# A two-layer graph transformer in one pipeline: value products and output projections of two units in one run in every second step

## The reference

```python
# layer 0
nx = ln(x, ln1_g, ln1_b); q, k, v = nx @ wq + bq, nx @ wk + bk, nx @ wv + bv
scores = q @ k.T / sqrt(32) + where(adj > 0, 0.1 * adj * adj, -inf)
out = softmax(scores) @ v
x1 = x + (out @ wo + bo)
x2 = x1 + gelu(ln(x1, ln2_g, ln2_b) @ w1 + b1) @ w2 + b2
# layer 1
q, k, v = x2 @ Wq + bq, x2 @ Wk + bk, x2 @ Wv + bv
h = softmax(where(adj == 0, -inf, q @ k.T / sqrt(32))) @ v
y = ln(h @ Wo + bo + x2, gamma, beta)
```

## Time and profile before

| what | value |
|---|---|
| median of 3 runs | 2196.2 us (2194.52 to 2197.47) |
| profiled execution, its own time | 2197.36 us |
| its span in the profile | 2195.3 us |
| mean granted TensorE clock | 0.988 |
| busy: PE, PEld, DVE, ACT, POOL | 2150.0, 1859.5, 1802.1, 1683.8, 1155.7 us |

### The profile page before, as it was taken

How to read it: one execution, slowest core, us unless ns; L and a number is a source line. 1 busy time by engine, 2 the same in 40 slices (tenths; PEclk the granted TensorE clock), 3 DMA queues, 4 the chain that set the end, 5 groups by cost and what they waited for, 6 DMA issues and landing times.

```text
span 2195.3 us, 58908 instructions
## 1 busy us (share of the span) xinstructions
PE 2150.0 (98%) x20300; PEld 1859.5 (85%) x20300; DVE 1802.1 (82%) x8414; ACT 1683.8 (77%) x5646; POOL 1155.7 (53%) x1266
## 2 busy tenths in 40 slices
PE   8899999999999999999999999999999999999986
PEld 6688888888888888888888888888888888888875
DVE  6688888888888888888888888888888888888774
ACT  5578787778777778877778877788877787877773
POOL 4345655445655455655455555455555455555454
PEclk9999999999999999999999999999999999999997
DMA  4010111011111001111101110101111001110000
GB/s 128 25 35 28 40 33 40 23 31 35 40 33 36 27 28 38 37 36 31 32 28 38 34 39 31 33 26 40 33 40 31 30 28 40 33 40 29 22 14 17
DMA packets 94309, 75.74 MB, mean 35 GB/s; under 512 B 8129, under 2 KB 93761, under 8 KB 94017
## 3 DMA queue, kind: packets, MB, share of 16 engines
q1 hardware_dynamic: 94016, 71.99, 10.7%
HBM read 55.20 MB, written 16.78 MB: 33 GB/s over the span
## 4 chain that ended last, share of the span: by engine, by line
PE 95%; DVE 2%; issue 1%; ACT 1%; POOL 0%; DMA 0%; SPq 0%; POOLq 0%; DVEq 0%
PE p_bank L1124 67%; PE p_heads L1221 10%; PE p_heads L1208 8%; PE p_bank L1240 7%; PE p_bank L1143 4%; ACT scores L650 1%; DVE normed L883 0%; DVE x_two L768 0%; DVE probs_t L920 0%; ACT normed L661 0%; DMA scores<-in_L_gnn_wk 0%; DVE scores L861 0%; DVE adj_c L814 0%; SPq L440 0%; POOL w_up L374 0%
## 5 line engine op out<-in xcount | busy, mean ns | idle before, releaser
L650 ACT ACTIVATE scores<-scores,negmax 128x128 f32<-128x128 f32 x2048 | 793.7, 393 | 25.4 <-DVE negmax L861 25.0
L585 POOL TENSOR_TENSOR scores<-scores,inverse 128x512 f32<-128x512 f32 x512 | 541.9, 1064 | 339.6 <-DVE inverse L872 339.6
L650 ACT ACTIVATION_READ_ACCUMULATOR scores<-scores,negmax 128x1 f32 x2048 | 392.2, 192 | 0.0
L1124 PEld LDWEIGHTS p_bank<-w_down,hidden 128*128 128x128 f32 x3072 | 374.7, 190 | 8.6 <-issue 6.0
L1124 PE MATMUL p_bank<-w_down,hidden 128*128 128x256 f32 x3072 | 381.8, 284 | 0.0
L1124 PE MATMUL p_bank<-normed,w_up 128*128 128x512 f32 x1536 | 370.3, 397 | 1.9 <-DVE normed L883 1.9
L1124 PEld LDWEIGHTS p_bank<-normed,w_up 128*128 128x128 f32 x1536 | 285.0, 189 | 67.6 <-issue 8.4
L1221 PE MATMUL p_heads<-ident,scores 128*128 128x128 f32 x2048 | 313.1, 276 | 8.3 <-DVE negmax L861 3.5
L861 DVE CUSTOM_DVE_ANT_0 scores<-p_heads,adj_a 128x128 f32<-128x128 f32 x1024 | 235.2, 286 | 43.7 <-issue 43.7
L1221 PEld LDWEIGHTS p_heads<-ident,scores 128*128 128x128 f32 x2048 | 241.2, 141 | 35.0 <-DVE negmax L861 11.1
L673 ACT ACTIVATE p_bank<-p_bank,ready_cols 128x512 f32<-128x512 f32 x256 | 169.5, 662 | 131.4 <-PE p_bank L1124 125.9
(11 more groups left out here) (117 smaller groups left out, 3704.5 us busy)
## 6 DMA issues: line engine op xcount, KB each, us to landing
res_a<-in_x SPq DMA_DIRECT2D x32, 512.0 KB, 3.8
out<-res_c SPq DMA_DIRECT2D x128, 128.0 KB, 1.7
x_in<-in_x SPq DMA_DIRECT2D x31, 512.0 KB, 3.8
adj_a<-in_adj SPq DMA_DIRECT2D x32, 256.0 KB, 2.9
adj_c<-in_adj SPq DMA_DIRECT2D x32, 256.0 KB, 2.9
piece_room<-in_L_gnn_w SPq DMA_DIRECT2D x2, 512.0 KB, 8.1
x_two<-in_x SPq DMA_DIRECT2D x1, 512.0 KB, 5.5
res_c<-in_L_gnn_w SPq DMA_DIRECT2D x1, 512.0 KB, 6.3
```

The source lines that it names most:

```text
L585: nc.gpsimd.tensor_tensor(rows_g, rows_g, inverse[:, step % 2, heads].unsqueeze(2).broadcast_to([P, HC, P]), ALU.mult).then_inc(probs_made, 1)
L650: last = nc.scalar.activation(scores[:, k % 2, h], scores[:, k % 2, h], ACT.Exp, scale=-1.0, bias=negmax[:, k % 2, h:h + 1], accum_out=tot ...
L1124: last = nc.tensor.matmul(dst, stationary(i), moving(j), start=(n == 0), stop=(n == total_n - 1))
```

## The change

Values and projections are no longer done in every step. In odd steps k, PE does V of the two units k - 3 and k - 2 in one run (16 matmuls, one PSUM bank) and W of the same two in one run (12 matmuls, one bank); in even steps neither. ACT's and DVE's splits, DVE's residual and POOL's deviation take both units in one instruction of twice the width, and `probs_t` and `heads_t` get room for two units. Normalization follows: for C the two rows of a pair in the step behind it; for A the rows 0 and 1 in steps 0 and 1, and rows 2 and 3 both in step 2, behind the second mask group. The tail behind the last step still works unit by unit. All matmuls stay the same in shape and number.

```diff
     by_step = {}
     for r, k in enumerate(steps):
-        by_step[k] = ([("V", r - 2), ("W", r - 2)] if r >= 2 or pending else []) + (
+        pair = [(r - 3, r - 2)] if r % 2 and (r >= 3 or pending) else []
+        by_step[k] = [("V", units) for units in pair] + [("W", units) for units in pair] + (
             [("T", r - 1)] if r >= 1 or pending else [])
     last = len(steps) - 1
-    tail = [("V", last - 1), ("T", last), ("W", last - 1), ("V", last), ("W", last)] if drain else []
+    tail = [("V", (last - 1,)), ("T", last), ("W", (last - 1,)), ("V", (last,)), ("W", (last,))] if drain else []
     return by_step, tail
...
-        self.late, waiting = {}, [-3] if pending else []
+        self.pending = pending
+        self.late, waiting = {}, []
...
-        probs_t = sb("probs_t", [P, H, P])
-        heads_t = sb("heads_t", [P, 2, KC, P], F32R)
+        probs_t = sb("probs_t", [P, 2, H, P])
+        heads_t = sb("heads_t", [P, 2, 2, KC, P], F32R)
...
             def rstd_of(t, ops):
-                for op, r in ops:
-                    if op == "W":
-                        _, stage, b = t.unit(r)
-                        make_rstd("M" if stage == "A" else "C", b, b + 1, (t.group(r) * GB + b) * 3 + 3)
+                for _, units in only("W", ops):
+                    _, stage, b = t.unit(units[0])
+                    make_rstd("M" if stage == "A" else "C", b, b + len(units), t.projection(units) * 3 + 3)
...
-            def heads_high(t, r):
-                bank, number = t.bank(("O", r))
+                nc.scalar.activation(turned_rows(r, 0), turned_columns(0), ACT.Copy).then_inc(turned_out0, 1)
+
+            def heads_high(t, units):
+                bank, number = t.bank(("O", units))
                 act.wait_ge(filled[bank], number)
-                nc.scalar.activation(heads_t[:, HI].rearrange("p c n -> p (c n)"), p_bank[bank][:, 0:KC * P],
+                nc.scalar.activation(heads_part(HI, units), p_bank[bank][:, 0:len(units) * KC * P],
                                      ACT.Copy).then_inc(high_made, 1)
...
-            def heads_low(t, r):
-                bank, _ = t.bank(("O", r))
-                dve.wait_ge(high_made, t.high(("O", r)))
-                part = lambda i: heads_t[:, i].rearrange("p c n -> p (c n)")
-                nc.vector.tensor_tensor(part(LO), p_bank[bank][:, 0:KC * P], part(HI).bitcast(F32), ALU.subtract
-                                        ).then_inc(drained[bank], 1)
-
-            def add_residual(t, r):
-
-                _, stage, b = t.unit(r)
-                bank, number = t.bank(("W", r))
+                nc.vector.tensor_copy(turned_rows(r, 1), turned_columns(1)).then_inc(turned_out1, 1)
+
+            def heads_low(t, units):
+                bank, _ = t.bank(("O", units))
+                dve.wait_ge(high_made, t.high(("O", units)))
+                nc.vector.tensor_tensor(heads_part(LO, units), p_bank[bank][:, 0:len(units) * KC * P],
+                                        heads_part(HI, units).bitcast(F32), ALU.subtract).then_inc(drained[bank], 1)
+
+            def add_residual(t, units):
+
+                _, stage, b = t.unit(units[0])
+                bank, number = t.bank(("W", units))
                 dve.wait_ge(filled[bank], number)
-                dve.wait_ge(biased[stage], t.group(r) * 2 + b // 2 + 1)
-                x = residual[stage]
-                nc.vector.tensor_tensor(x[:, b, :], p_bank[bank][:, 0:D], x[:, b, :], ALU.add
-                                        ).then_inc(drained[bank], 1)
-
-            def measure(t, r):
-
-                _, stage, b = t.unit(r)
-                bank, number = t.bank(("W", r))
+                dve.wait_ge(biased[stage], t.group(units[0]) * 2 + b // 2 + 1)
+                x = residual[stage][:, b:b + len(units), :].rearrange("p g n -> p (g n)")
+                nc.vector.tensor_tensor(x, p_bank[bank][:, 0:len(units) * D], x, ALU.add).then_inc(drained[bank], 1)
+
+            def measure(t, units):
+
+                _, stage, b = t.unit(units[0])
+                bank, number = t.bank(("W", units))
                 dve.wait_ge(drained[bank], number)
-                layer_norm_steps("M" if stage == "A" else "C", residual[stage], b, b + 1, (t.group(r) * GB + b) * 3)
-
-            def apply_norm(t, r, entry):
-
-                _, stage, b = t.unit(r)
-                group = t.group(r)
-                if stage == "C":
-                    normalize("C", res_c, res_c, b, b + 1, group * GB + b + 1)
-                elif entry is not None:
-                    wait(dve, biased["C"], group * 2 - (entry < 2))
-                    normalize("M", res_a, x_two, entry, entry + 1, group * GB + entry + 1)
+                layer_norm_steps("M" if stage == "A" else "C", residual[stage], b, b + len(units),
+                                 t.projection(units) * 3)
+
+            def finish_c(t, units):
+
+                if t.unit(units[0])[1] == "C":
+                    for r in units:
+                        b = t.unit(r)[2]
+                        normalize("C", res_c, res_c, b, b + 1, t.projection(units) + 1)
+
+            def normalize_m(t, entry, group, made):
+
+                wait(dve, biased["C"], group * 2 - (entry < 2))
+                normalize("M", res_a, x_two, entry, entry + 1, made)
...
-                    if k == 2:
-                        for r in s.late.get(k, []):
-                            apply_norm(t, r, GB - 1)
+                    if k == 2 and s.m and s.pending:
+                        normalize_m(t, 2, t.group_m, t.projections("A", 1))
+                        normalize_m(t, 3, t.group_m, t.projections("A", 1))
                     if k in s.units and k != s.behind:
                         invert(t, k, 0)
-                    for r in s.late.get(k, []):
-                        if k != 2:
-                            apply_norm(t, r, {0: 0, 1: 1}.get(k))
+                    for units in s.late.get(k, []):
+                        finish_c(t, units)
+                    if k < 2 and s.m and s.pending:
+                        normalize_m(t, k, t.group_m, t.projections("A", 0))
...
-                    if k == 1:
-                        for r in s.late.get(k, []):
-                            apply_norm(t, r, 2)
...
+            def value_products(t, units):
+
+                bank, dst = take(t, ("O", units))
+                u_last, stage, _ = t.unit(units[-1])
+                pe.wait_ge(turned_out0, u_last + 1)
+                pe.wait_ge(turned_out1, u_last + 1)
+                if t.unit(units[0])[2] == 0:
+                    for i in range(2):
+                        pe.wait_ge(*drained_bank(*made(t, "V", stage, i)))
+                for i, r in enumerate(units):
+                    _, _, b = t.unit(r)
+                    for h in range(H):
+
+                        j, c = h % HC, h // HC
+                        last = nc.tensor.matmul(dst[HD * j:HD * (j + 1), (i * KC + c) * P:(i * KC + c + 1) * P],
+                                                values[room(t, stage)][:, b, h * HD:(h + 1) * HD],
+                                                probs_t[:, parity(r), slot_of(c, j), :], start=True, stop=True)
+                last.then_inc(filled[bank], 1)
+
...
+            def project(t, units):
+
+                bank, number = t.bank(("O", units))
+                pe.wait_ge(drained[bank], number)
+                bank, dst = take(t, ("W", units))
+                w = weight[weights_of[t.unit(units[0])[1]][3]]
+                for at_unit in range(len(units)):
+                    last = three_passes(dst[:, at_unit * D:(at_unit + 1) * D], [
+                        (lambda i, c=c: heads_t[:, i, at_unit, c, :], lambda j, c=c: w[:, j, c, :])
+                        for c in range(KC)])
+                last.then_inc(filled[bank], 1)
```

69 lines of the change are left out of this document (32 added, 37 removed).

## The result

The changed kernel takes 2282.18 us in the median of five runs (2280.86 to 2284.20), the kernel before 2197.47 in the same job (2194.52 to 2202.69): a ratio of 1.0383, 95% interval 1.0366 to 1.0399. The profiled execution has a span of 2282.0 us where that of before has 2195.3, 86.7 more. Slower was forecast, but by 30 us and not by 85; the time lies far outside the range.

The account below looks back on a forecast made before the run. PE was taken to bound the kernel; waits of 1.70 less savings of .74 us a turn, over 30 turns, gave 28.8, plus 1.5 at the ends: 30.3 us more, 2226.5 us in the runs' measure, range 2213 to 2236.

Parts of the forecast that it names:

- The bound and the period: Whole kernel: PE is 95% of the chain that ended last, and a turn repeats every 66.11 us.
- What PE saves: PE's paired V runs: .16 us a pair, plus .10 in front of step 5's K product, .74 us a turn.
- W saves nothing: PE's projections: paired W with the even step's adjacent turns loses 0 to .08 us a pair, taken as 0.
- The second turns' waits: PE in steps 2, 6 and 0 waits for the last four heads' probabilities: .50, .50 and .70, 1.70 us a turn.
- the half DOWN product of 5.86 us covers it: Step 4: the half DOWN product hides the second turn's wait, so no wait there.
- Edits at nothing: ACT, POOL and DVE's wider instructions, the banks and step 2's later normalizations: put at no effect on PE's time.
- The ends: Last turn's finishing costs 1.5 us more; starved steps of turns 0, 1, 32 and 33 put at 0, within 3.
- The shared port: DVE and POOL in step 2: first normalization ends at 3.10, .06 late; the full blocking rule would make XT .25 late.
- Rival 3: A second wait joins, on step 2's XT, odd steps' W or masks of steps 2 and 6: 9 to 15 us more, chance .13.

Follow-up runs that it names:

- E1: Changed kernel, but in step 4 DVE normalizes C's rows 0 and 1 behind the turned copy and the measuring; 2271.95 us, ratio 1.0339.
- E7: Changed kernel with C's pair normalized behind the turned copy in steps 4 and 6, and SP's res_a load ahead of the row 0 and 1 stores; 2239.10 us.
- E8: E7 plus, on DVE in steps 0, 2 and 6, the reciprocal of the last four heads ahead of the first mask group; 2214.31 us.
- E13: E8 with other PE work between the two turns: second K half in step 0, second Q half in step 6, x_two's transposes in step 2; 2265.45 us.
- E16: E5 with the res_a load first, plus POOL reordered: step 0's last-four-heads product before both biases, step 5's finish behind step 6's products; 2255.45 us.
- E5: Changed kernel with the projection of a pair's second unit moved to the next even step, between the turns of steps 4, 6, 0; 2432.44 us.

## Why the prediction was wrong

By its own steps:

- **The bound and the period.** Right: PE, 66.11 us a turn.
- **What PE saves.** Right, .74 forecast and .66 measured for the value products, in which the gap in front of step 5's K is counted. The guess it leaned on holds: scores directly in front of a product last .66, as in front of V. "W saves nothing" is right as a sum: the paired projections save .32, the adjacent turns cost about as much (.87 for eight transposes where two runs of four took .35 + .44).
- **The second turns' waits.** Right: forecast .50, .50 and .70 in steps 6, 2 and 0; measured .49 (1070.04 less 1067.00 is 3.04, less the 2.55 that PE needs), .46 and .61, that is 1.56 a turn for 1.70.
- **Step 4: "the half DOWN product of 5.86 us covers it", and "Edits at nothing".** This is the step that failed: the path of x_two in step 4 was put at nothing. That the product covers it is true of the second turn, and I asked of nothing else in step 4; XT was timed for step 2 only. In step 4 the turn doesn't wait, so PE comes to the transposes 1.29 us earlier and finds .35 of slack instead of 1.07. The row that would have said how little room there was stood in the trace of the kernel before: DVE's x_two of step 4 ends 1.07 us before PE needs it. Under "Edits at nothing" what VectorE does was looked at in the odd step, in step 2 and at the last turn, but not the pair of C rows that the code also finishes in steps 4 and 6. In step 4 it makes VectorE's queue end 1.02 us later, and the transposes behind it wait 1.14 us a turn, 34 us; in step 6 it delays the turned copy, and step 7's scores wait .30: 9 us. E1 shows the first: without the pair in front of x_two that wait is gone.
- **The ends.** Forecast 1.5, within 3; measured 12. Three starved stretches lost about 4 us each. By which waits was not followed further, and it stays open.
- **The shared port.** The prediction took the row with .16 left after POOL's end as speaking against the rule's full size. It is the rule's ordinary case: every normalization that meets POOL ends .15 after it. For step 2 the row gave the right time (first normalization forecast to end 3.10 behind the scores, measured 3.09). For the two of step 4, which met a product and took 1.43, it wasn't used.

In sum, by the table: value products, projections and turns 30 x (1.83 - .66 - .32) = 25.5, where 29 were forecast; transposes 35; Q with step 7's scores 9; K and V projection 6.5, of which step 1's scores, .09 a turn later than before, are about 3 and the rest was not followed; the ends 12. That is 88, where the spans differ by 87 and the medians by 85. Rival 3, "a second wait joins", named the right kind of thing in the wrong places and at a third of its price at most (9 to 15 us, against 43 for the transposes and step 7's scores).

The experiments bear this out as far as they go: E7 takes away step 4's and step 7's waits and gives 43 us, E8 also shortens the second turns' and gives 68, both without touching the pairs. What is left of E8's 17 us is about 10 in the turns, where the second turns of steps 0 and 2 still wait .2 to .4, and 7 at the ends. Neither other work between the turns (E13) nor POOL's order (E16) recovers it. No version here beats the kernel before.

## What to carry to other kernels

When work is taken out of a step, follow every later instruction of the step that waits for another engine, not just the one next to the hole: each arrives earlier by the whole saving. Its slack is a number that the trace of before shows, and what it waits for must be followed back too: the part that hangs on the shortened engine comes earlier with it, the part that stands in another engine's queue does not, and any instruction that the change adds to that queue counts in full. When a result is finished later, read the queues of all the engines behind it, the DMA issuer's too: here a late store held a load, the load held GpSimd, and GpSimd held TensorE. And a filling that seems movable may be hiding something behind it (E13): before moving it, read who needs the result of the run in front of it.

## What the runs showed of the hardware

In E5 the granted clock of TensorE fell during a wait of 4.6 us (1.00 until 1132, .51 in the rest of it) and stood at .50 for the 3.7 us behind it, so that the six products there took 2.91 and not 1.64 us.

A row normalization on VectorE takes .38 to .41 us unless it meets GpSimd; 243 of the 384 in the kernel after take longer, and each ends .146 to .154 us after an instruction of GpSimd. GpSimd's product takes 1.09 to 1.14 us when a normalization was already running at its start (122 cases) and 1.03 to 1.05 otherwise (390). Two normalizations took .73 with GpSimd idle until near their end (E1) and 1.43 beside its product; four took 2.08 with one of them beside a product (E1) and 3.20 with each beside an instruction of GpSimd.
